# Adaptive feed-forward kernel: tiles in five stretches, one x sum on VectorE, contiguous projection rows

## What is computed

```python
q = relu(cond @ W3 + b3)                           # 32 x 512
x1 = (64 * x + sum(x, axis=1)) * q[:, None, :]     # per batch
h0 = relu(x1 @ W2 + b2)                            # 2048 rows x 512
h = square(relu(h0 @ ternary(W_fc).T))             # 2048 x 2048
hn = h * rsqrt(mean(h * h, axis=-1) + eps)
out = x + hn @ ternary(W_proj).T                   # 2048 x 512
```

## Time and profile before

| | us |
|---|---|
| median of 3 runs | 323.41 |
| lowest, highest | 322.25, 323.43 |
| the profiled execution | 322.98 |
| its span in the trace | 321.0 |
| PE busy | 315.2 (98%) |
| DVE, ACT, POOL busy | 210.6, 192.3, 112.9 |

### The profile page before, as it was taken

One profiled execution on the slowest core, in us unless ns is written; L12 is line 12 of the kernel. 1 busy time (PEld: TensorE's weight loads), 2 busy tenths in 40 slices (PEclk: granted clock), 3 DMA queues, 4 the chain that ended last, 5 costly groups with the idle time before them and its releaser, 6 DMA issues.

```text
span 321.0 us, 3855 instructions
## 1 busy us (share of the span) xinstructions
PE 315.2 (98%) x1336; PEld 239.8 (75%) x1336; DVE 210.6 (66%) x290; ACT 192.3 (60%) x282; POOL 112.9 (35%) x94
## 2 busy tenths in 40 slices
PE   8999999999999999999999999999999999999995
PEld 7764554644888788888888888888888888888884
DVE  0447989798998856577555565855565575665545
ACT  1639898799996876444555444554445554445550
POOL 1003333334553435414334441334443314443330
PEclk9999999999999999999999999999999999999999
DMA  6993959678731110007000000510000015000003
GB/s 190 300 315 84 267 157 255 172 146 263 130 52 34 33 36 1 0 0 263 0 0 2 0 0 0 198 68 0 2 0 0 0 64 199 0 0 2 0 1 132
DMA packets 31331, 27.02 MB, mean 84 GB/s; under 512 B 18736, under 2 KB 20816, under 8 KB 31312
## 3 DMA queue, kind: packets, MB, share of 16 engines
q1 hardware_dynamic: 29984, 26.25, 29.8%
q10 hardware_dynamic: 1328, 0.53, 0.6%
HBM read 18.39 MB, written 4.19 MB: 70 GB/s over the span
## 4 chain that ended last, share of the span: by engine, by line
PE 69%; ACT 10%; DVE 7%; issue 7%; DMA 5%; SPq 0%; POOL 0%; DVEq 0%; ACTq 0%; POOLq 0%
PE ps_out L321 34%; PE ps_acc L308 31%; DMA w_turned<-w_tern 3%; DVE abs_sum L412 3%; DMA raw<-in_L_ffn_W_proj_dram 3%; DVE x_t L439 2%; ACT w_scale L532 2%; ACT h_f L554 2%; PE ps_acc L363 1%; ACT x_t L562 1%; ACT w_abs L526 1%; ACT x_t L559 1%; PE ps_out L273 1%; ACT w_t L539 1%; ACT w_sign L527 1%
## 5 line engine op out<-in xcount | busy, mean ns | idle before, releaser
L210 POOL TENSOR_TENSOR wv_sb<-wv_sb 128x512 f32<-128x512 f32 x55 | 82.2, 1494 | 113.9 <-ACT wv_sb L565 113.9
L321 PE MATMUL ps_out<-w_t,y_hi 128*128 128x512 f32 x256 | 101.7, 397 | 0.2 <-DVE y_lo L454 0.2
L321 PE MATMUL ps_out<-w_t,y_lo 128*128 128x512 f32 x256 | 100.9, 394 | 0.0
L308 PE MATMUL ps_acc<-h_hi,w_t 128*128 128x512 f32 x256 | 100.1, 391 | 0.0
L308 PE MATMUL ps_acc<-h_lo,w_t 128*128 128x512 f32 x256 | 100.0, 391 | 0.0
L454 DVE TENSOR_TENSOR y_lo<-x_t,y_hi 128x512 fp32r<-128x512 f32 x64 | 91.3, 1427 | 2.2
L559 ACT ACTIVATE x_t<-ps_acc 128x512 f32<-128x512 f32 x64 | 38.1, 595 | 81.0 <-PE ps_acc L308 81.0
L452 DVE CAST y_hi<-x_t 128x512 fp32r<-128x512 f32 x64 | 29.5, 461 | 73.2 <-PE ps_out L321 65.7
L321 PEld LDWEIGHTS ps_out<-w_t,y_hi 128*128 128x128 f32 x256 | 48.1, 188 | 11.7 <-DVE y_lo L454 0.6
L321 PEld LDWEIGHTS ps_out<-w_t,y_lo 128*128 128x128 f32 x256 | 48.3, 189 | 10.9
L308 PEld LDWEIGHTS ps_acc<-h_hi,w_t 128*128 128x128 f32 x256 | 48.3, 189 | 10.6 <-issue 0.2
(11 more groups left out here) (48 smaller groups left out, 148.7 us busy)
## 6 DMA issues: line engine op xcount, KB each, us to landing
x_sb<-in_x_dram SPq DMA_DIRECT2D x7, 1024.0 KB, 6.3
raw<-in_L_ffn_W_fc_dram SPq DMA_DIRECT2D x8, 512.0 KB, 5.7
raw<-in_L_ffn_W_proj_dram SPq DMA_DIRECT2D x8, 512.0 KB, 6.1
out_dram<-x_t SPq DMA_DIRECT2D x16, 256.0 KB, 2.5
x_sb<-in_x_dram SPq DMA_DIRECT2D x4, 256.0 KB, 5.6
wv_sb<-in_L_cond_W_dram SPq DMA_DIRECT2D x4, 256.0 KB, 7.2
x_t<-in_L_cond_W_dram ACTq DMA_DIRECT2D x1, 512.0 KB, 4.9
w_turned<-w_tern SPq DMA_TRANSPOSE x16, 3.1
```

What stands on the lines that cost most here:

```text
L210: engine.tensor_tensor(sq_acc[:], sq_acc[:], y_sq[:, v % SQ_RING, :], ALU.add).then_inc(sq_added, 1)
L308: last = pe.matmul(ps_acc[:, (UNITS + v) % ACC_RING, :], w_t[:, j, k * P:(k + 1) * P], part[:, k, g * BANK:(g + 1) * BANK], start=(k == 0 ...
L321: last = pe.matmul(ps_out[:, t, :], part[:, v % RING, t * P:(t + 1) * P], w, start=(j == 0 and part is y_hi), stop=(j == HJ - 1 and part i ...
```

## The change

The tiles run in five stretches: blocks 0 to 7 of group 0, all of group 1, blocks 8 to 15 of group 0, then groups 2 and 3. At the end of the first stretch DVE copies group 0's partial products out of `ps_out` (`set_aside`) and at the end of the third adds the new ones (`merge`) and, in four further instructions, the residual (`add_residual`). The sums of squares have two accumulators. Results are written over the residual in `x_res` and stored from there; a later residual is loaded only when the stores before it are done. The steps of the weights are spread further: ten instead of twelve in the unit stage.

The sums of group 3 are no longer in PE's product: PE transposes x with the identity (16 `pe.transpose`), at the start of group 2's units (ahead of unit 8 instead of 10), and DVE adds the batch sums in three instructions per block. `load_x(3)` moves to behind `turn_pair(3)`, `load_x(2)` ahead of `turn_pair(0)`.

In the start the warm-up is 5 products, and the products for q stand between the second and third quarter of group 0's sums. `keep_pair` stores w_proj so that the moving operand of `project` is one run of 512.

```diff
-WARM_UP = 10
+WARM_UP = 5
+    STRETCHES = [(0, 0, HJ // 2), (1, 0, HJ), (0, HJ // 2, HJ), (2, 0, HJ), (3, 0, HJ)]
-    STEP_AT_UNIT = {0: 0, 1: 1, 3: 2, 4: 3, 5: 4, 7: 5, 8: 6, 9: 7, 11: 8, 12: 9, 13: 10, 15: 11}
-    STEP_AT_TILE = {1: 12, 3: 13, 5: 14, 7: 15}
-    KEEP_AT_TILE = {8: 14, 9: 15}
+    STEP_AT_UNIT = {1: 0, 3: 1, 4: 2, 5: 3, 7: 4, 9: 5, 11: 6, 12: 7, 13: 8, 15: 9}
+    STEP_AT_TILE = {0: 10, 3: 11, 6: 12, 9: 13, 12: 14, 15: 15}
+    KEEP_AT_TILE = {16: 14, 17: 15}
...
                 if i + RAW_RING + 1 < len(PAIRS):
                     load_pair(i + RAW_RING + 1)
+                if i == 0:
+                    load_x(2)
                 turn_pair(i)
-                if i == 1:
-                    load_x(2)
-                if i == 4:
+                if i == 3:
                     load_x(3)
...
-                        last = sum_x_block(t, k)
+                        if sums_by_vector(g):
+                            last = pe.transpose(ps_out[:, k, t * P:(t + 1) * P], x_sb[:, t, k * P:(k + 1) * P], ident_f[:])
+                        else:
+                            last = sum_x_block(t, k)
...
-                w = w_t[:, HJ + KD * c:HJ + KD * (c + 1), i * P:(i + 1) * P]
+                w = w_t[:, HJ + j, :]
...
             for u in range(UNITS):
-                if u % KD == SUMS_AT and u // KD + 1 < GROUPS:
+                if u % KD == SUMS_AT and u // KD + 1 < GROUPS - 1:
                     sum_x(u // KD + 1)
+                if u == KD * (GROUPS - 2):
+                    sum_x(GROUPS - 1)
                 make_h0(u)
...
+                if sums_by_vector(g):
+                    at = 2 * k
+                    wait(dve, summed, at)
+                    dve.tensor_reduce(batch_sum[:], src, AX.X, ALU.add).then_inc(summed, 1)
+                    dve.wait_ge(summed, at + 1)
+                    dve.scalar_tensor_tensor(out=x1, in0=src, scalar=float(N),
+                                             in1=batch_sum[:].rearrange("p (b o) -> p b o", o=1).to_broadcast([P, GB, N]),
+                                             op0=ALU.mult, op1=ALU.add).then_inc(summed, 1)
+                    dve.wait_ge(summed, at + 2)
+                    src = x1
...
+                if g == GROUPS - 2:
+                    scale_x(g + 1, m)
```

More of the change, by code:

```diff
@@ L60, in adaln_ffn, with opens, closes @@
     assert D == BANK and GROUPS == 4 and TT == 4 and KD == 4
+    STRETCHES = [(0, 0, HJ // 2), (1, 0, HJ), (0, HJ // 2, HJ), (2, 0, HJ), (3, 0, HJ)]
+    TILE_AT = [(r, g, j) for r, (g, first, end) in enumerate(STRETCHES) for j in range(first, end)]
+    START = [sum(end - first for _, first, end in STRETCHES[:r]) for r in range(len(STRETCHES) + 1)]
+    def opens(v):
+        return v in START
+    def closes(v):
+        return v + 1 in START
     def fc_pair(a):
@@ L196, in projected_at @@
         def projected_at(v):
-            g, j = v // HJ, v % HJ
-            return (tile_summed, TT * (g + 1)) if j == HJ - 1 else (projected, (HJ - 1) * g + j + 1)
+            r, g, j = TILE_AT[v]
+            return (tile_summed, TT * (r + 1)) if closes(v) else (projected, v + 1 - r)
         def add_squares(engine, v):
-            g, j = v // HJ, v % HJ
+            r, g, j = TILE_AT[v]
+            acc = sq_acc[:, g % 2, :]
             engine.wait_ge(sq_ready, v + 1)
             if j == 1:
-                wait(engine, part_summed, g)
-                engine.tensor_tensor(sq_acc[:], y_sq[:, (v - 1) % SQ_RING, :], y_sq[:, v % SQ_RING, :], ALU.add
+                if g > 1:
+                    engine.wait_ge(part_summed, 4 - g)
+                engine.tensor_tensor(acc, y_sq[:, (v - 1) % SQ_RING, :], y_sq[:, v % SQ_RING, :], ALU.add
                                      ).then_inc(sq_added, 2)
@@ L209, in add_squares @@
                 engine.wait_ge(sq_added, v)
-                engine.tensor_tensor(sq_acc[:], sq_acc[:], y_sq[:, v % SQ_RING, :], ALU.add).then_inc(sq_added, 1)
+                engine.tensor_tensor(acc, acc, y_sq[:, v % SQ_RING, :], ALU.add).then_inc(sq_added, 1)
         @block.sync
@@ L313, in project_tile @@
             def project_tile(v, t):
-                g, j = v // HJ, v % HJ
-                c, i = j // TT, j % TT
-                w = w_t[:, HJ + KD * c:HJ + KD * (c + 1), i * P:(i + 1) * P]
-                if j == 0:
-                    wait(pe, finished, TT * (g - 1) + t + 1)
+                r, g, j = TILE_AT[v]
+                w = w_t[:, HJ + j, :]
+                if opens(v):
+                    wait(pe, finished, TT * (r - 1) + t + 1)
                 for part in (y_hi, y_lo):
                     last = pe.matmul(ps_out[:, t, :], part[:, v % RING, t * P:(t + 1) * P], w,
-                                     start=(j == 0 and part is y_hi), stop=(j == HJ - 1 and part is y_lo))
-                if j == HJ - 1:
+                                     start=(opens(v) and part is y_hi), stop=(closes(v) and part is y_lo))
+                if closes(v):
                     last.then_inc(tile_summed, 1)
@@ L370, in _ @@
                 pe.matmul(ps_acc[:, 1, 0:P], ident_f[:], ident_f[:], start=True, stop=True)
[L371 to L377, removed]
             pe.wait_ge(consts_ready, 1)
             for t in range(TT):
+                if t == TT // 2:
+                    pe.wait_ge(condt_ready, 1)
+                    pe.wait_ge(wq_loaded, 16)
+                    for m in range(KD):
+                        for k in range(KQ):
+                            last = pe.matmul(ps_x[:, m * BATCHES:(m + 1) * BATCHES], wq_sb[:, k, m * P:(m + 1) * P],
+                                             cond_t[:, k, :], start=(k == 0), stop=(k == KQ - 1))
+                    last.then_inc(q_done, 1)
                 pe.wait_ge(x0_loaded[t], 16)
@@ L454, in split_y, with sum_parts, inverse_root @@
                 dve.tensor_tensor(y_lo[:, v % RING, :], y[:, v % RING, :], y_hi[:, v % RING, :], ALU.subtract).then_inc(split, 1)
[L456 to L460, removed]
+            def sum_parts(r):
+                acc = sq_acc[:, STRETCHES[r][0] % 2, :]
+                dve.wait_ge(sq_added, START[r + 1])
+                wait(dve, sq_summed, r - 1)
+                dve.tensor_reduce(part_sq[:], acc.rearrange("p (j b) -> p j b", b=QUAD), AX.X, ALU.add,
                                   apply_transpose=True).then_inc(part_summed, 1)
[L463 to L465 removed]
+            def inverse_root(r):
+                dve.wait_ge(sq_summed, r)
+                if r == GROUPS:
                     dve.tensor_scalar(mean_sq[:], ps_sq[:, 0:TT], 1.0 / H, RMS_EPS, ALU.mult, ALU.add).then_inc(mean_ready, P // QUAD)
[L467 removed]
+                for q in range(P // QUAD if r < GROUPS else 0):
                     rows = slice(q * QUAD, (q + 1) * QUAD)
@@ L486, in finish, with merge @@
                 for t in range(TT):
-                    dve.wait_ge(tile_summed, TT * g + t + 1)
-                    dve.scalar_tensor_tensor(out=o_sb[:, t, :], in0=ps_out[:, t, :], scalar=rstd[:, t:t + 1],
-                                             in1=x_res[:, t, :], op0=ALU.mult, op1=ALU.add).then_inc(finished, 1)
+                    dve.wait_ge(tile_summed, t + 1)
+                    dve.tensor_copy(partial[:, t, :], ps_out[:, t, :]).then_inc(finished, 1)
+            def merge(r):
+                inverse_root(r)
+                for t in range(TT):
+                    dve.wait_ge(finished, t + 1)
+                    dve.wait_ge(tile_summed, TT * r + t + 1)
+                    dve.tensor_tensor(partial[:, t, :], ps_out[:, t, :], partial[:, t, :], ALU.add).then_inc(finished, 1)
@@ new lines, in add_residual, with finish @@
+            def add_residual(r):
+                dve.wait_ge(rstd_ready, r)
+                dve.wait_ge(res_loaded, 16 * r)
+                dve.wait_ge(finished, TT * (r + 1))
+                for t in range(TT):
+                    dve.scalar_tensor_tensor(out=x_res[:, t, :], in0=partial[:, t, :], scalar=rstd[:, t:t + 1],
+                                             in1=x_res[:, t, :], op0=ALU.mult, op1=ALU.add).then_inc(merged, 1)
+            def finish(r):
+                inverse_root(r)
+                dve.wait_ge(rstd_ready, r)
+                dve.wait_ge(res_loaded, 16 * r)
+                for t in range(TT):
+                    dve.wait_ge(tile_summed, TT * r + t + 1)
+                    dve.scalar_tensor_tensor(out=x_res[:, t, :], in0=ps_out[:, t, :], scalar=rstd[:, t:t + 1],
+                                             in1=x_res[:, t, :], op0=ALU.mult, op1=ALU.add).then_inc(finished, 1)
@@ L491, in _, with read_out @@
+            def read_out(r):
+                if r == 0:
+                    set_aside()
+                elif STRETCHES[r][0] == 0:
+                    merge(r)
+                else:
+                    finish(r)
             dve.wait_ge(condt_done, 1)
```

117 lines of the change are left out of this document (66 added, 51 removed).

## The result

The changed kernel takes 332.92 us (median of 4 runs, 332.25 to 333.72) against 323.42 for the kernel before: ratio 1.0306, 95% interval 1.028 to 1.0332. The profiled execution took 332.25 (span 330.5).

A forecast was written before the change was run, and what follows sets the result against it. PE, busy 98% of the span, was taken to bound the kernel. From the profiled 322.98 us, -1.1 - 0.2 - 2.6 - 1.8 + 5.7 + 2.9 + 3.0 = +5.9 gave 328.9 us; the range was 322.5 to 332.0.

The forecast's parts named there:

- Projection rows contiguous: -2.6: In the tiles: one operand run instead of four saves `project` 0.04 us in each of 64 tiles, 2.6 us.
- the layout does nothing: Rival for the tiles: the layout of w_proj is not what slows `project`, so no 2.6 gain; 331.5 us, chance 0.12.
- the 0.45 for spreading the steps: Units and first tiles: spreading the weights' steps over more tiles can return PE some 0.45 us.
- Start: -1.1, -0.2: Kernel start: group 0's sums begin before q's products, -1.1 us; earlier `load_x(2)` removes the wait before group 2's sums, -0.2.
- Sums of group 3: -1.8: PE in the unit stage: 16 transposes are 16 records in place of 32, saving 1.8 us.
- The x of group 3: +5.7: Ahead of unit 8: `load_x(3)`, behind `turn_pair(3)`, is issued 3.25 us after unit 6 ends; PE waits 5.7 us.
- The rival that had x in time: Ahead of unit 8: load issued before unit 6 has run a third, no wait or cold clock; 320.2 us, chance 0.12.
- The clock: +3.0: After PE's wait for group 3's x: PE runs at 1.2 in place of 2.4 GHz for a while, losing 3.0 us.
- DVE and ACT behind it: +2.9: Tiles 0 and 1: DVE's added instructions and the steps delay `project` by 2.1 and 1.3, 3.4 less 0.45.
- At 0: Extra stretch boundary, DVE's copies, merges, residual adds, stores and later residuals: covered by other work, costing 0 us.

The follow-up runs named there:

- the last of the shifts: The kernel before with 32 unused bytes ahead of `w_t`, so that `w_t` and y move together and `h0` stays: 325.1 us.
- the early load: The changed kernel with `load_x(3)` issued ahead of `turn_pair(3)` in SP's queue: 324.43 us, ratio 1.0043.
- the old four runs: The changed kernel with the old layout of w_proj, four runs per operand of `project`: 333.77 us.
- `batch_sum` last: The changed kernel with only the 32 bytes of `batch_sum` allocated last: 330.35 us, ratio 1.0243.
- sums on PE again: The changed kernel with the early load, group 3's sums back in PE's product and one DVE instruction per block instead of three: 323.69 us.
- three repairs: The changed kernel with the early load, `batch_sum` allocated last, and one weight step fewer among the units, later ones moved: 318.73 us, ratio 0.9872.

## Why the prediction was wrong

The sum can be read in three stretches of the two timelines. Each number is a difference between the starts of the changed kernel and of the one before, where these rows start the first `hidden`, `project` of tiles 0 and 1, and the last two projects:

```profile
79.15 0.79 PE L308 MATMUL ps_acc<-h_hi,w_t 128*128 128x512 f32 x1
...
85.05 0.39 PE L321 MATMUL ps_out<-w_t,y_hi 128*128 128x512 f32 x1
...
88.75 0.40 PE L321 MATMUL ps_out<-w_t,y_hi 128*128 128x512 f32 x1
...
308.84 0.40 PE L321 MATMUL ps_out<-w_t,y_hi 128*128 128x512 f32 x1
```

In the changed kernel the last of them is

```profile
318.36 0.39 PE L349 MATMUL ps_out<-w_t,y_hi 128*128 128x512 f32 x1
```

| to | forecast | measured |
|---|---|---|
| the first `hidden` | -1.1 - 0.2 - 1.8 + 5.7 + 3.0 = +5.6 | 83.46 - 79.15 = +4.3 |
| from there to `project` of tile 1 | +3.4 | 12.83 - 9.60 = +3.2 |
| from there to the last two projects | -2.6 - 0.45 = -3.05 | 222.07 - 220.09 = +2.0 |
| sum | +5.9 | +9.5 |

**The step that failed is "Projection rows contiguous: -2.6".** It took the 0.04 between `project` and `hidden` for the price of four runs. Contiguous rows alone gained nothing: the run with them was 0.3 us slower, with an interval across no change. What the 0.04 comes from stays open. Four banks or one may be the cause, but the last of the shifts shows `hidden`, which writes one bank, at 1.86 too, by the place of its operands; no run moved the operands of `project` until it took 1.82. The rival "the layout does nothing" had this right. The Trainium skill, "Advanced Engine Details and Errata", section "Memory Cachelines", would have it so as well; the ratio of 1.001 agrees for runs of 512 bytes.

The rival's 331.5 is still short, because the prediction put one edit at nothing without listing it: the 32 bytes for `batch_sum`, which added 2.30 on the same stretch (222.07 - 219.77). The two together, 2.6 that were not gained and 2.3 that were added, are the 5 us by which the third line of the table is off; the 0.45 for spreading the steps is left with about 0.3 (220.09 - 219.77).

**Start: -1.1, -0.2.** Right in sign, too small for this trace: by the units after the sums of group 2 the gain is 41.65 - 39.48 = 2.17. Of this 1.58 lies ahead of the first unit, which began at 13.24 before and at 11.66 now, and 0.6 around the sums of group 2, where only 0.20 had been named as a wait. The second quarter waited for nothing, and all 16 records of the first half took 7.65 - 5.32 = 2.33, where I had counted 2.9 with a wait for x in between. This is partly luck: in the trace with the early load the same 16 records took 3.16 (5.33 to 8.49) without a named wait, and units began 0.85 later than in this one (40.33 against 39.48).

**Sums of group 3: -1.8.** Right: 1.75 at the full clock for what took 39.48 - 35.91 = 3.57 on the products of group 2.

**The x of group 3: +5.7.** Right, by the chain it named: issued 3.20 after unit 6, forecast 3.25; PE's wait 5.86. The rival that had x in time named the point that decides, a load before unit 6 is a third done; with the early load SP issued it at 40.53, where unit 6 began at 40.33, and the wait was gone.

**The clock: +3.0.** Right, at the upper end of what three traces show: it cost 2.27 by the starts in the changed kernel's trace, where the low clock lasted through the transposes (3.47 for 1.75) and 1.1 us of unit 8 (0.55). Two other traces have the same wait. From the first transpose to the first `hidden` the one with the old four runs took 84.89 - 53.08 = 31.81 and the one with `batch_sum` last 83.94 - 52.36 = 31.58, against 28.82 with the early load: 3.0 and 2.8. So the price differs from execution to execution. It had been taken from the kernel's start with a slip: the 18 records set beside the first 26 in the earlier trace rows are not the same matmuls, since 16 of them are the products for q with 32 columns.

```profile
7.43 1.87 PE L375 MATMUL ps_x<-h_f,x_t 128*128 128x32 f32 x16
```

The 0.112 of the sums from 9.14 on, which are 128x128 like the warm-up, carries the 3.0 all the same. The Trainium skill, "TensorE: Matmul & The Clock Gate", section "HAM oscillation — how this bites in real kernels", says that a wait for DMA between bursts of matmuls can put the clock back; the granted clock of 0.50 here agrees.

**DVE and ACT behind it: +2.9.** Right: 3.2 at tiles 0 and 1, forecast 3.4. DVE's instructions took 0.69 each, as bounded. Tile 0's 2.2 is the sum of them and of the steps in front: it goes when the additional instructions go (sums on PE again), and also when they stay and the steps are moved (three repairs). Tile 1's 1.0 goes, but for 0.1, only with the steps. That ACT's step 10 alone makes tile 1 late is argued, since the run that moved it moved others too.

**At 0:** the stretches, copies and merges did cost nothing: with `batch_sum` last and nothing else mended, the way from `project` of tile 1 to the last two takes 219.77, against 220.09 before.

## What to carry to other kernels

A difference of 2% between two streams of products is no evidence for the one cause that the edit touches; try that cause alone first. When a load moves in a queue's program, follow what it stands behind to the engine that releases it: here one line moved up was worth 8 us. And a new small tile belongs behind the large ones in the allocation, or the pace of unrelated products has to be looked at again.

## What was not expected of the hardware

The pace of PE's fp32r products depends on where their operands lie in SBUF relative to each other. With the same instructions a tile's 16 products took 3.68 us as placed before and with everything shifted together, and 3.71 to 3.73 with y 32 bytes up, y 64 bytes down, `y_lo` alone 32 bytes up, or `w_t` and y 32 bytes up. Moving y, with small tiles that PE's tile does not read, slowed `hidden`, which does not read y either (1.82 to 1.85), so it is not simply the address that a product reads; whether it meets the other engines' traffic in SBUF was not tried.

The granted clock read 1.00 at the kernel's start, although the 128x128 products there took about 0.23 us a record and 0.112 to 0.119 from 9.14 on the earlier trace rows. It did show the fall in the middle: 0.53 and 0.50.
